# Two attentions with values and ones in one matmul, small norm steps on GpSimd, and another written order, in an eight-stage transformer kernel on one core

## The reference

```
L0 attention: 16 heads of 8; q, k, v pass a spiking neuron (values 0 to 4 of 4), y = softmax(q k^T) v, then W_o
L0 ffn:       FP4-quantised gated MLP, 128 -> 352 -> 128
L1 attention: 4 Mamba layers (conv of 4, state 16, scan over the 256 tokens), gated by silu(z)
L1 ffn:       128 -> 512 -> 512 -> 512 -> 128, silu gate and two gelus
L2 attention: causal linear attention, phi(x) = elu(x) + 1;
              y = (tril(phi(q) phi(k)^T) v) / (its row sums + 1e-6), then W_proj
L2 ffn:       8 experts, each token takes the output of its top one
L3 attention: decaying convolution, gelu, projection, a second layernorm
L3 ffn:       dense MLP + top-8 of 64 key products over 512 experts, softmax and silu weights
```

## Time and profile before

| | |
|---|---|
| median of 3 runs | 2051.56 us (2051.1 to 2055.4) |
| the profiled execution's own time | 2051.34 us |
| its span, first to last instruction | 2049.4 us |
| busy DVE / PE / ACT / POOL | 1702.0 / 1507.7 / 1306.8 / 1175.3 us |
| mean granted TensorE clock | 0.852 of full |

### The profile page before, as it was taken

The page is one execution under the profiler, slowest core; times in us unless marked ns, Lnnn a source line. Parts: engine busy times, 40 slices in busy tenths (PEclk is TensorE's granted clock), DMA queues, the critical chain, the costliest instruction groups (busy, mean ns, idle before and its releaser), DMA issues.

```text
span 2049.4 us, 29431 instructions
## 1 busy us (share of the span) xinstructions
PE 1507.7 (74%) x9897; PEld 1057.2 (52%) x9897; DVE 1702.0 (83%) x2868; ACT 1306.8 (64%) x2676; POOL 1175.3 (57%) x1342
## 2 busy tenths in 40 slices
PE   5777666667788887566766888767887786779975
PEld 2343333334566655444445666545665554567755
DVE  6489899998988889989988887899988989973266
ACT  3466565656767676675576767778777666554453
POOL 3038476766667676655756665566666666650023
PEclk8777777767988998797798999988898998899986
DMA  4023414333443443221243434332335542112300
GB/s 178 1 63 78 92 33 90 85 78 83 109 109 89 119 104 89 65 56 41 59 113 99 106 104 112 93 91 69 85 105 119 143 110 54 48 39 83 108 16 6
DMA packets 69238, 170.39 MB, mean 83 GB/s; under 512 B 14561, under 2 KB 19937, under 8 KB 64609
## 3 DMA queue, kind: packets, MB, share of 16 engines
q1 hardware_dynamic: 69088, 168.52, 32.4%
HBM read 99.26 MB, written 2.10 MB: 49 GB/s over the span
## 4 chain that ended last, share of the span: by engine, by line
DVE 34%; PE 25%; ACT 19%; issue 8%; POOL 6%; SPq 4%; DMA 4%; DVEq 0%; POOLq 0%; ACTq 0%
DVE m L981 12%; ACT m L959 6%; DVE dtuB L973 5%; POOL m L992 5%; SPq L935 4%; DMA m<-m 3%; PE ps L1388 2%; PE ps L1395 2%; ACT L345 2%; PE ps L1107 2%; PE ps L646 2%; PE ps L1236 2%; PE ps L1680 2%; PE ps L1005 1%; DVE o L1539 1%
## 5 line engine op out<-in xcount | busy, mean ns | idle before, releaser
L992 POOL TENSOR_TENSOR m<-m 128x256 f32<-128x256 f32 x1024 | 938.0, 948 | 339.4 <-DVE m L981 339.1
L981 DVE TENSOR_TENSOR_SCAN m<-m,dtuB 128x1024 f32<-128x1024 f32 x256 | 584.3, 2282 | 21.9 <-ACT m L959 3.2
L959 ACT ACTIVATE m<-m,Aneg 128x256 f32<-128x256 f32 x1024 | 432.0, 497 | 117.7 <-DMA m<-m 79.1
L973 DVE TENSOR_TENSOR dtuB<-m 128x1024 f32<-128x1024 f32 x256 | 340.4, 1330 | 21.2 <-DMA m<-m 16.8
L1005 PE MATMUL ps<-m,w_const 128*32 128x256 f32 x2048 | 167.5, 427 | 49.0 <-POOL m L992 48.9
L1388 PE MATMUL ps<-o 128*128 128x256 f32 x512 | 159.6, 422 | 37.8 <-DVE X L1332 23.9
L366 POOL TENSOR_TENSOR o<-o,mhalf 128x2 f32<-128x2 f32 x64 | 48.1, 752 | 230.8 <-DVE o L358 229.6
L1355 ACT ACTIVATE o<-ps,w_mo 128x256 f32<-128x256 f32 x256 | 113.8, 469 | 85.9 <-PE ps L1388 84.8
L1395 PE MATMUL ps<-o 128*128 128x128 f32 x1024 | 137.8, 291 | 13.4 <-ACT o L1355 11.0
L1107 PE MATMUL ps<-o 128*128 128x256 f32 x512 | 130.5, 406 | 19.1 <-ACT o L1076 17.6
L1395 PEld LDWEIGHTS ps<-o 128*128 128x128 f32 x1024 | 131.1, 206 | 25.7 <-issue 22.0
(11 more groups left out here) (242 smaller groups left out, 2922.3 us busy)
## 6 DMA issues: line engine op xcount, KB each, us to landing
m<-m SPq DMA_DIRECT2D x512, 128.0 KB, 2.5
m<-spread SPq DMA_DIRECT2D x128, 256.0 KB, 4.6
o<-in_mox SPq DMA_DIRECT2D x128, 256.0 KB, 2.7
o<-in_l1x SPq DMA_DIRECT2D x88, 256.0 KB, 3.0
w_mb<-in_mb SPq DMA_DIRECT2D x1, 2288.0 KB, 12.3
m<-in_cwr SPq DMA_DIRECT2D x1, 2048.0 KB, 16.2
w_l3f<-in_l3f SPq DMA_DIRECT2D x1, 1536.0 KB, 17.6
X<-in_x SPq DMA_DIRECT2D x4, 256.0 KB, 6.8
```

The source lines that it names most:

```text
L959: op = e.activation(dA[at % NA][:, j, :], R[q][:, h, 0, :], ACT.Exp, scale=Aneg[:, l, 4 * g + j:4 * g + j + 1])
L973: e.tensor_tensor(dtuB[:, :, :], bc(R[q][:, h, 1, :].unsqueeze(1), 4, CH), Br[k % 2], ALU.mult).then_inc(S.dve, n.tick(f"b{g}"))
L981: e.tensor_tensor_scan(flat(G[at % NG]), flat(dA[at % NA]), flat(dtuB[:, :, :]), 0.0, ALU.mult, ALU.add).then_inc(S.dve, n.tick(f"s{g}"))
L992: op = e.tensor_tensor(part, part, Cr[k % 2][:, j:j + 1, :], ALU.mult)
```

## The change

The attentions put a head's 8 value columns and 8 columns of ones side by side in one 32-wide weight tile, so that one matmul gives numerator and denominator. The result, features by tokens, is copied to SBUF by ACT, turned by four transposes, divided on DVE with one reciprocal per head and token (128 x 32), turned back by two transposes and copied by ACT (`divide_act`, `divide_pe`, `divide_dve`). The rows of both output weights are permuted on the host to match (`by_pair`). In `L2Attn` ACT reads phi's input from PSUM for both exp and relu, DVE does the rest in one instruction, and k is masked four times per chunk and not 16, the scores' matmuls reading 32 rows of it. The norms' small steps all go to POOL, as three more instructions of 128x2. `Front` makes z after dt, on PE and ACT; the use of z waits for it. `L1Ffn` and `L2Ffn` end in a sum whose k loop is outermost, so that only its last two matmuls wait for the last block. `L3Ffn` makes the four product tiles in one instruction and lets ACT scale and sum the silu by `accum_out`. The 5 strings of `ORDER` are new.

```diff
 ORDER = {
     "dve":
-        "a2ua7u2bubub7a12bafbafbfabfb3a7b5fbsfbsfbsfsfs5b7s5fs6fsf2sfs10af2a2sf2asfasa2s6asasa3fs2a2sas3ba4baba2bfb2fbfsf"
...
+        "aua7u2b8u2a11bafafb4a2ba5b4fbsb2fs2fs2bs2b6s3fs11fsf2s2as5a2sa3bs2afa4fsbfbfa2s5asas2asa2sa2fs9fsf2s8bfs4as3a2fb2"
...
             e.wait_ge(T.dve, n.dve(f"{p}mv1"))
-            e.tensor_scalar(v.ve, v.mv[:, :, 1], EPS, None, ALU.add).then_inc(T.dve, n.tick(f"{p}ve"))
-            yield
+            e.tensor_tensor(v.ve, v.mv[:, :, 1], mhalf[:, 2:4], ALU.add).then_inc(T.pool, n.tick(f"{p}ve"))
+            e.tensor_tensor(v.nb, v.mv[:, :, 0], mhalf[:, 4:6], ALU.mult).then_inc(T.pool, n.tick(f"{p}ng"))
+            e.wait_ge(T.pool, n.pool(f"{p}ve"))
+            e.tensor_tensor(v.rs, v.ve, mhalf[:, 0:2], ALU.pow).then_inc(T.pool, n.tick(f"{p}rs"))
             e.wait_ge(T.pool, n.pool(f"{p}rs"))
-            e.scalar_tensor_tensor(v.nb, v.mv[:, :, 0], -1.0, v.rs, ALU.mult, ALU.mult).then_inc(T.dve, n.tick(f"{p}nb"))
-            yield
-
-        def norm_pool(e, n, T, v, p=""):
-            e.wait_ge(T.dve, n.dve(f"{p}ve"))
-            e.tensor_tensor(v.rs, v.ve, mhalf[:, :], ALU.pow).then_inc(T.pool, n.tick(f"{p}rs"))
+            e.tensor_tensor(v.nb, v.nb, v.rs, ALU.mult).then_inc(T.pool, n.tick(f"{p}nb"))
 
         def norm_act(e, n, T, v, src, dst, p=""):
-            e.wait_ge(T.dve, n.dve(f"{p}nb"))
+            e.wait_ge(T.pool, n.pool(f"{p}nb"))
...
         def spread_pool(e, n, T, v):
             v4 = v.rearrange("p i (g j e) -> p i g j e", g=4, j=4)
             for j in range(4):
-                e.tensor_copy(T.vz[:, :, j, :].rearrange("p i (g j e) -> p i g j e", g=4, j=4)[:, :, :, j, :],
+                e.tensor_copy(T.vz[:, :, j, :].rearrange("p i (g x) -> p i g x", g=4)[:, :, :, 8 * (j % 2):8 * (j % 2) + 8],
                               v4[:, :, :, j, :]).then_inc(T.pool, n.tick(f"vz{j}"))
+        def divide_act(e, n, T, b, v, what):
+            e.copy(v.zs, b[:, :]).then_inc(T.act, n.tick("zs"))
+            yield
+            e.wait_ge(T.pe, n.pe("yt"))
+            e.copy(v.yT, b[:, 0:CH]).then_inc(T.act, n.tick("yT"))
...
+        def divide_pe(e, n, T, b, other, v):
+            e.wait_ge(T.act, n.act("zs"))
+            for t in range(2):
+                for k in range(2):
+                    op = e.transpose(other[:, cut(2 * t + k)], v.zs[:, (2 * k + t) * 128:(2 * k + t) * 128 + 128], ident)
+            op.then_inc(T.pe, n.tick("zt"))
+            yield
+            e.wait_ge(T.dve, n.dve("y"))
+            for t in range(2):
+                op = e.transpose(b[:, cut(t)], v.yn[:, cut(t)], ident)
+            op.then_inc(T.pe, n.tick("yt"))
+            yield
+            e.wait_ge(T.act, n.act("yT"))
+        def divide_dve(e, n, T, other, v, number, op):
+            all_ = other[:, :].rearrange("p (k s j e) -> p k s j e", s=2, j=2, e=8)
+            e.wait_ge(T.pe, n.pe("zt"))
+            e.tensor_scalar(v.dn, all_[:, :, 1, :, 0], number, None, op).then_inc(T.dve, n.tick("dn"))
+            e.wait_ge(T.dve, n.dve("dn"))
+            e.reciprocal(v.dr, v.dn).then_inc(T.dve, n.tick("dr"))
+            e.wait_ge(T.dve, n.dve("dr"))
+            e.tensor_tensor(v.yn.rearrange("p (k j e) -> p k j e", j=2, e=8), all_[:, :, 0, :, :],
+                            bc(v.dr.unsqueeze(3), 16, 2, 8), ALU.mult).then_inc(T.dve, n.tick("y"))
+            yield
...
+                        op = e.memset(T.vz[:, :, j, :].rearrange("p i (g x) -> p i g x", g=4)[:, :, :, at:at + 8], 1.0)
...
+                yield from divide_act(e, n, T, T.banks[1], v, "z33")
...
-                        for what in range(2):
-                            for g in range(4):
-                                lhs = T.vz[:, kt, j, 32 * g:32 * g + 32] if what == 0 else ones4[:, j, :]
-                                op = e.matmul(z[32 * g:32 * g + 32, what * CH:what * CH + CH], lhs, v.Pr[g][:, kt * CH:kt * CH + CH],
-                                              start=(j == 0 and kt == 0 and what == 0), stop=(j == 3 and kt == 1),
-                                              skip_group_check=True)
-                                if kt == 1 and what == 1:
-                                    op.then_inc(T.pe, n.tick(f"z{j}{g}"))
-                    yield
-                e.wait_ge(T.dve, n.dve("y"))
+                        for g in range(4):
+                            op = e.matmul(z[32 * g:32 * g + 32, j // 2 * CH:j // 2 * CH + CH], T.vz[:, kt, j, 32 * g:32 * g + 32],
+                                          v.Pr[g][:, kt * CH:kt * CH + CH], start=j == 0 and kt == 0, stop=j % 2 == 1 and kt == 1,
+                                          skip_group_check=True)
+                            if kt == 1:
+                                op.then_inc(T.pe, n.tick(f"z{j}{g}"))
+                    yield
+                yield from divide_pe(e, n, T, z, a, v)
...
+                    e.wait_ge(F.act, F.at(k - 2, "act", "z"))
...
+                e.wait_ge(F.pe, n.pe("wz"))
+                table(e, "silu")
+                e.activation(v.z, halves_of(b), ACT.Silu).then_inc(F.act, n.tick("z"))
+                yield
...
+                e.wait_ge(F.dve, n.dve("dt"))
+                for h in range(2):
+                    op = e.matmul(b[:, h * CH:h * CH + CH], m("win", l)[:, 256 + h * 128:384 + h * 128], v.xT[:, 3:3 + CH],
+                                  start=True, stop=True)
+                op.then_inc(F.pe, n.tick("wz"))
...
-                e.wait_ge(T.act, n.act("h23"))
-                for i in range(2):
-                    for k in range(4):
...
+                for k in range(4):
+                    if k in (0, 3):
+                        e.wait_ge(T.act, n.act(f"h2{max(k, 2)}"))
+                    for i in range(2):
+                        op = e.matmul(T.banks[1][:, cut(i)], v.ha[:, k, cut(i)], v.ring[10 % RING][:, cut(k)],
+                                      start=k == 0 and i == 0, stop=k == 3, skip_group_check=True)
...
-                    src, out = T.banks[b][:, 0:size], {"q": v.qT, "k": v.kT, "t": v.kt}[name]
-                    e.wait_ge(T.pe, n.pe(name))
-                    e.tensor_scalar(v.mn[:, 0:size], src, 0.0, None, ALU.min).then_inc(T.dve, n.tick(f"m{name}"))
-                    yield
-                    e.wait_ge(T.act, n.act(f"e{name}"))
-                    e.scalar_tensor_tensor(out, src, 0.0, v.ex[:, 0:size], ALU.max, ALU.add).then_inc(T.dve, n.tick(name))
+                    out = {"q": v.qT, "k": v.kT, "t": v.kt}[name]
+                    e.wait_ge(T.act, n.act(f"p{name}"))
+                    e.scalar_tensor_tensor(out, v.ex[name], 1.0, out, ALU.min, ALU.add).then_inc(T.dve, n.tick(name))
                     yield
...
-                e.wait_ge(T.pe, n.pe("z33"))
-                e.tensor_scalar(v.mn, T.banks[0][:, CH:2 * CH], 1e-6, None, ALU.add).then_inc(T.dve, n.tick("dn"))
-                e.wait_ge(T.dve, n.dve("dn"))
-                e.reciprocal(v.ex, v.mn).then_inc(T.dve, n.tick("r"))
-                e.wait_ge(T.dve, n.dve("r"))
-                e.tensor_tensor(v.xT, T.banks[0][:, 0:CH], v.ex, ALU.mult).then_inc(T.dve, n.tick("y"))
-                yield
+                yield from divide_dve(e, n, T, T.banks[1], v, 1e-6, ALU.add)
...
-                    e.wait_ge(T.dve, n.dve(f"m{name}"))
+                    src, out = T.banks[b][:, 0:size], {"q": v.qT, "k": v.kT, "t": v.kt}[name]
+                    e.wait_ge(T.pe, n.pe(name))
                     table(e, "exp")
-                    e.activation(v.ex[:, 0:size], v.mn[:, 0:size], ACT.Exp).then_inc(T.act, n.tick(f"e{name}"))
+                    e.activation(v.ex[name], src, ACT.Exp).then_inc(T.act, n.tick(f"e{name}"))
+                    e.activation(out, src, ACT.Relu).then_inc(T.act, n.tick(f"p{name}"))
                     yield
...
-                for p in range(8):
-                    for i in range(2):
-                        h = 4 * (2 * (p % 2) + i) + p // 2
-                        if p:
-                            e.wait_ge(T.pe, n.pe(f"s{p - 1}"))
-                        e.activation(v.km[i], v.kT, ACT.Identity, scale=hm[:, h:h + 1]).then_inc(T.act, n.tick(f"k{p}{i}"))
-                    yield
+                e.wait_ge(T.dve, n.dve("k"))
+                for h in range(4):
+                    e.activation(v.km[h], v.kT, ACT.Identity, scale=hj[:, h:h + 1]).then_inc(T.act, n.tick(f"k{h}"))
+                    if h % 2:
+                        yield
+                yield from divide_act(e, n, T, T.banks[0], v, "z7")
...
+                    g = slice(32 * (p % 4), 32 * (p % 4) + 32)
                     for i in range(2):
-                        e.wait_ge(T.act, n.act(f"k{p}{i}"))
+                        e.wait_ge(T.act, n.act(f"k{2 * (p // 4) + i}"))
                         for t in range(2):
-                            op = e.matmul(b[:, i * CH + t * 128:i * CH + t * 128 + 128], v.km[i][:, cut(t)], v.qT[:, cut(t)],
```

(42 more changed lines are left out.)

169 lines of the change are left out of this document (84 added, 85 removed).

## The result

The changed kernel takes 2093.32 us (2088.77 to 2100.09, 4 runs). The kernel before took 2051.1, 2051.56 and 2055.4 beside it; a fourth run of it, at 2429.78, was a slow one and is left out of the ratio. The ratio is 1.0201, with a 95% interval of 1.0163 to 1.0238: the changed kernel is about 2% slower. The prediction was 1973, and its range ended at 2044. The profiled execution took 2088.77 us, 4.6 less than the median, and its mean granted clock is 0.826, where the kernel before has 0.852.

A forecast was written before the change was run, and what follows sets the result against it. The prediction took DVE, 89% busy, to bound the middle (the 32 scan units). Head 112.6, middle 1631 (DVE busy 1436, idle 195), tail 228 and 1.9 around them gave 1973 us, range 1905 to 2044.

The forecast's parts named there:

- 179 + 19 - 3: DVE's idle time in the middle: 179 before, 19 more from table loads, 3 less from z behind dt, 195 us.
- Rival F: Whole kernel: the order gives back what the edits save, by an unseen static wait, within 4 us of before; chance 0.03.
- less 1.6 in the two L2 attentions: In the tail: 1.6 us taken off the matmul time that PE gets there from shifted work.
- PE, -52: PE's busy time: L646 halves, -59.1, L1248 goes, -20.2, transposes add 27.6; net -52 us, the middle's part slack.
- DVE, -91, of which -71 in the middle: DVE's busy time: 110.5 us removed, 19.4 added, net -91; head -6, tail -14, middle -71.
- POOL, +62 and hidden: 312 more small norm instructions on POOL at 0.2 us each, +62 us (31 to 215), hidden behind the scans.
- Rival D: Each of the 312 small POOL instructions stops DVE for its 0.2 us where DVE is busy: 2026 us; chance 0.04.
- Table loads: ACT: 236 loads for 170, +85 us of ACT; a quarter reaches DVE's idle in the middle, +19 us.
- Rival A: All added table loads, 77 us in the middle and 5 in the head, delay DVE: 2036 us; chance 0.12.
- z behind dt, -3 and -1.5: Shorter chain to the scan's DMAs: -3 us of idle in the middle (bounds 0 and -30), -1.5 in the head.
- Head -13: Until the first scan unit: halved L646 blocks -10.9, division +2.5, L0 ffn about -3, with z -13, to 112.6 us.
- Tail +3: Last stretch: PE's shifted matmuls +13, L3 ffn -6, L2 attention -4; +3, 228 us; growth over 15 would show error.

The follow-up runs named there:

- e17: The changed kernel with e12's SP list and L2 attention's scores reading 128 rows with the change's own four masks; 2017.25 us, ratio 0.9825.
- e12: The changed kernel with only SP's list altered: in six units the transfers spreading B and C go before the scan's rows; 2046.68 us, ratio 0.9979.
- e1: All edits of the change, but in the order of the kernel before, new turns where they first can run; 2086.06 us, ratio 1.0177.
- e2: The changed kernel in its own order, L2 attention's score matmuls reading 128 rows and not 32; 2061.77 us, ratio 1.0043.
- e11: The kernel before with half of the scan's output matmuls (1024 of 2048) left out; 2054.36 us, ratio 1.0004.
- e6: The kernel before, its order less vanished turns, with only the norms' small steps moved to GpSimd; 2046.00 us, ratio 0.9965.
- e10: The kernel before with DVE's product of the scan cut to half its columns from the second group on; 2008.98 us, ratio 0.9772.
- e7: The kernel before, its order less vanished turns, with only the edits to L3 ffn and the k loops of L1 and L2 ffn; 2063.18 us, ratio 1.0048.
- e18: The kernel before with 64 more table loads put on ACT, two in each of the 32 scan units; 2081.53 us, ratio 1.0137.
- e4: The kernel before with only z moved behind dt, in the order of before; 2075.32 us, ratio 1.0106.
- e14: e13 with z back ahead of dt in PE's and ACT's lists, the rest of the order unchanged; 2110.15 us.
- e13: e12 with L2 attention's scores reading all 128 rows and one mask for each of the 16 heads; 2034.37 us, ratio 0.9901.
- e5: The kernel before, own order, with only L2 attention's score matmuls narrowed to 32 of 128 rows; 2074.89 us, ratio 1.0122.
- e9: The kernel before with only L0 attention's score matmuls widened to read all 128 rows and not 32; 2044.56 us, ratio 0.9961.
- e16: e13 with L0 attention's scores reading all 128 rows too, the edit of e9; 2024.11 us, ratio 0.9859.

## Why the prediction was wrong, point by point

The miss is 120 us. In the terms of the sum, the profiled execution is 115 over: 65 are DVE's idle time in the middle (195 forecast, 259.7 measured), 8 its busy time there (1436, 1444.1), 34 the tail (228, 262.3) and 8 the head (112.6, 120.8). So the term that failed first is the idle time, "179 + 19 - 3". By experiment, 47 us are SP's order and 29 to 32 the narrow scores. The last 44 lie between e17 (2017) and 1973.

**The step that failed first: the order.** I counted table loads along the list, and did not read SP's. Rival F ("by a static wait I do not see") had 0.03 and no row behind it. The wait was there to be seen in the new list: a letter s ahead of the f that stands for the spread. It is the only fault of the new list that a run has shown (PE's wait for L2 ffn's weights is a second suspect): with it mended the new order is 39 us ahead of before's order for the same edits (e12 and e1).

**The second: "less 1.6 in the two L2 attentions", and nothing for the narrow scores.** The edit from 128 to 32 rows I took for free on PE. For the single matmul that was right, at either level of the clock (2.4 and 1.2 GHz): the minimum, median and maximum (ns) of the changed kernel's

```profile
L1274 PE MATMUL ps<-o x512: 270/270/578, 544.3 to 1929.0; 32*128 32x128 f32 x171
```

are 271, 275 and 583 ns for L1236 before. But more of them, and of the matmuls around, ran at the lower level, so the mean rose:

```profile
L1274 PE MATMUL ps<-o 32*128 32x128 f32 x512 | 89.3, 323 | 18.1 <-DVE o L1198 17.9
L1285 PE MATMUL ps<-o,o_vz 128*32 128x128 f32 x512 | 43.4, 325 | 3.3 <-DVE o L1198 3.3
L683 PE MATMUL ps<-o,o_vz 128*32 128x256 f32 x512 | 53.9, 555 | 19.6 <-ACT o L644 19.6
```

and the same two L2 groups in e2, which differs in the rows alone:

```profile
L1274 PE MATMUL ps<-o 128*128 128x128 f32 x512 | 77.3, 298 | 22.7 <-DVE o L1198 22.6
L1285 PE MATMUL ps<-o,o_vz 128*32 128x128 f32 x512 | 37.2, 292 | 2.9 <-DVE o L1198 2.8
```

**PE, -52.** L646 halves as forecast, 118.2 to 53.9. L1248's 20.2 us go too, but L1245, whose 512 entries of 128x128 were busy for 21.2 us, comes back as L1285, with the same 512 and the same shape, busy for 43.4. In the code a block of 16 goes through four column groups in turn there, through two here, and a block takes 0.65 us (at 571.79 in the kernel before) and 1.07 (at 558.72): with medians of 273 ns in both, more of them overlapped there. The clock isn't it, since e17 still has 35.5 us at a mean of 282 ns. I took its time over unchanged, so that part of the -52 was nothing. And e11 says what such a term is worth: 1024 matmuls less gave no time, while the clock fell. PE's +51.6 us in place of -52 falls to -0.6 in e17 (1507.1, with the same count of matmuls).

**DVE, -91, of which -71 in the middle.** The sizes of the steps were near: L3 ffn's new product L1560 0.463 us (0.43), the reciprocal L454 0.353 (0.35). The sum over the removed steps is wrong, though: its terms give 117.1 us and not 110.5, so the net is -98. Measured is -86.1. The slip brought the forecast nearer by luck, and phi's last step was to stay at its size and did not: L1185 takes 0.584 and 0.416 us where L1145 took 0.414 and 0.284, 3.4 us in all.

What failed is the reading of the earlier trace rows as "DVE is the bound there", for the order as it was. DVE's 89% is the share of an engine whose list is woven with four others; taken away there, 36.1 us gave 7 (e6), 139.6 gave 43 (e10), 22.5 gave minus 10 (e7). Of these only e10 takes nothing but DVE's work away (POOL's products got shorter with it); e6 adds to POOL, and e7 moves matmuls. In the order made for the edits the reading does better. e17's middle, without the two costs, is 51 us shorter than before (1648.3) for 74 us less of DVE (1446.4), with 201.9 us idle where I had 195. So what the sum missed in the middle is mostly the two costs, and 17 us are left.

**POOL, +62 and hidden.** The three added steps take 76.9 us (0.26 and 0.35, 0.19, 0.24 and 0.28 each, by tile), within the bounds. POOL as a whole comes to 1206.8 (near 1240), since its products of the scan are busy 30.4 us less than before (907.6) and the powers 8.8 less. Hidden fits e6. Rival D is not seen in e6 either: 312 small POOL instructions, and DVE's scans stay at a mean of 2282 ns, its products go from 1330 to 1322.

**Table loads.** The count is 237 (236; and 171 in the kernel before, where I counted 170), the waits for exps 13.3 us (under 25). The share that comes through was too low: a quarter, +19; by e18 about half, which for 66 loads (85 us) makes some 41. Rival A's full price is refuted too.

**z behind dt, -3 and -1.5.** Alone +22 (e4): 53 loads more come with it, 68 us of ACT, and half of that would be 34. By that reckoning, which no run tests, z's own steps gain at most some 12. In the new order z ahead of dt is no choice (e14), though there the list stays as it was made for the other.

**Head -13, measured -4.7.** In the kernel before three of the eight blocks of L646 in the head (from 59.05, 65.28 and 74.73 us) had all or part of their matmuls at the upper level of the clock; in the changed kernel seven of eight stand like this:

```profile
33.13 1.93 PE L683 MATMUL ps<-o,o_vz 128*32 128x256 f32 x16 [0.84 <-ACT o L644]
34.99 0.60 PE L675 MATMUL ps<-o 32*128 32x256 bf16 x2
```

A pair of scores takes 0.60 us at the lower level and 0.39 at the upper. So the halved blocks lost part of their gain: 1.93 us each where 1.8 was forecast, and 1.07 in one only. The stretch's granted clock doesn't tell this. It is 0.80 before and 0.75 here, but 0.66 in e13, 0.86 in e12 and 0.91 in e17, which have the same list in the head, seven of eight blocks at 1.93 or 1.94 us, and heads of 118.5 to 120.3 us. The 0.9 us for four more hops had no row behind it. By what else the head is longer no run tells.

**Tail +3, measured +37.7**, which I had named as a sign of being wrong. PE is busy 33.2 us longer there at a clock of 0.86 (0.91). The two repairs take it from 262.3 to 258.0 (e12) and to 248.7 (e17: 1766.8 to 2015.5), so 21 of the 44 us still open are here and 17 in e17's middle (1648.3, forecast 1631), 6 in its head (118.5). The loads' 22 us over my term would account for half of these 44; that is arithmetic, not a run.

## What to carry to other kernels

A busy share of 89% doesn't make an engine the bound where fixed lists tie five engines together, and what its time is worth changes with the order: leave out a piece of its work alone, once, and see what comes through, before a sum is made one for one. Read every queue's list in a diff of an order, SP's above all, for a transfer that another one's consumer needs: two letters exchanged in six places cost 47 us, more than the 34 that all the edits cost in before's order (e1). An edit and the order made for it are worth something together and can be a loss apart, so a part taken back in a foreign order doesn't tell its price. Matmuls made smaller so that PE has less to do can pay with the clock of their neighbours.

## What the runs showed of the hardware that was not expected

**Fewer rows, lower clock.** In four pairs that differ in the rows of the score matmuls alone, with the same count and columns (the kernel before and e5 differ in that way and in which head is masked), the granted clock went with the rows: 0.826 and 0.839 (e2), 0.852 and 0.842 (e5, narrow), 0.852 and 0.862 (e9), 0.844 and 0.863 (e12, e17), and the time with it by 32, 24, 8 and 29 us. One execution's clock can mislead, as the head showed, but the means over all runs agree (0.827 and 0.848, 0.850 and 0.838, 0.850 and 0.860, 0.840 and 0.860), and so does PE's busy time for the same matmuls: 1559.3 and 1526.0 us, 1507.7 and 1541.1, 1507.7 and 1490.0, 1545.7 and 1507.1. e16 adds 10 us to e13 (0.848, 0.853). Half the output matmuls less (e11) took the clock to 0.830. The Trainium skill (TensorE: Matmul & The Clock Gate, "What's actually happening") says that the clock's gate opens and closes with how busy PE has been. e11 agrees. The four pairs add that score matmuls of 32 rows, which keep PE busy as long, leave more of what runs around them at 1.2 GHz and less at 2.4. Why they do, no run shows.

**DVE's product holds up POOL's.** POOL's products of the scan in the kernel before, and in e10, where DVE's product has half the columns (min/median/max ns):

```profile
L992 POOL TENSOR_TENSOR m<-m x1024: 712/726/1791, 130.8 to 1827.0; 128x256 f32<-128x256 f32 x171
```

```profile
L993 POOL TENSOR_TENSOR m<-m x1024: 712/726/1372, 129.4 to 1786.1; 128x256 f32<-128x256 f32 x171
```

Median and minimum stay; the longest falls by 419 ns, and the mean from 948 to 836, 115 us over the 1024. DVE's product went from a median of 1234 ns to 701, by 533. DVE's product may be held up in its turn, in the kernel before:

```profile
L973 DVE TENSOR_TENSOR dtuB<-m x256: 1216/1234/1839, 125.6 to 1821.2; 128x1024 f32<-128x1024 f32 x128
```

Its mean is 1330 ns, 96 over the median, and its longest is 605 over. The Trainium skill (SBUF — State Buffer, "SBUF: two separate sides") has it that a DVE instruction with two inputs from SBUF and a GpSimd instruction that reads SBUF exclude each other for a whole instruction. The rows agree for this pair: POOL's products wait, by experiment; that DVE's wait for POOL's is read from the mean alone. The rows don't agree for DVE's scan, which reads two tiles of SBUF as well: from 710.22 us eight of POOL's products took 7.54 us in the kernel before while two scans of 2.29 and 2.27 us ran (from 711.54 and 715.56). At 712 ns each the eight take 5.7, so neither scan held them for its length. That DVE's product holds up POOL's was the direction that my rival D didn't look at.
